# First x rows as four loads, per-channel constants turned by PE, and products ahead of PE's first projection

## The reference, cut to what matters

```python
# x: [4, 512, 512], ctx: [4, 512, 256]; DI = 512 channels, DS = 16 states, DC = 4 taps
z   = layernorm(x)                                   # used as the gate, per row
xi  = einsum('ed,bld->bel', in_proj_w, ctx)          # in-projection
xc  = depthwise_conv(xi, conv_w, 4 taps)             # taps: conv_w [512, 4]
u   = silu(xc + conv_b[None, :, None])
xdbl = einsum('ke,bel->bkl', x_proj_w, u)            # rows: dt_lo 16, B 16, C 16
delta = softplus(einsum('er,brl->bel', dt_proj_w, dt_lo) + dt_proj_b)
A = -exp(A_log)
# for each step t: state = state * exp(delta_t * A) + delta_t * u_t * B_t;  y_t = sum_n state * C_t
y = (y + D * u) * silu(z)
x = x + swapaxes(y, 1, 2)
# then x + ffn(layernorm(x)), with weights rounded to -1, 0, 1 by their mean and rows rounded to 8 bits
```

## Time and profile before

| what | value |
|---|---|
| time, median of 3 runs (range) | 584.99 us (584.41 to 585.54) |
| the profiled execution's own time | 586.31 us |
| its span, first to last instruction | 584.4 us |
| mean granted TensorE clock | 0.991 |
| busy: PE, DVE, ACT, POOL | 541.3, 540.5, 512.1, 464.5 us |
| chain that ended last, by engine | DVE 28%, PE 26%, ACT 17%, POOL 12%, issue 11%, DMA 5% |
| DMA busy share in the first four of 40 slices (14.6 us each), in tenths | 9, 9, 9, 2 |
| packets under 512 bytes | 41136 of 62194 |

### The profile page before, as it was taken

One profiled execution on the slowest core, in us unless ns is written; L12 is line 12 of the kernel. 1 busy time (PEld: TensorE's weight loads), 2 busy tenths in 40 slices (PEclk: granted clock), 3 DMA queues, 4 the chain that ended last, 5 costly groups with the idle time before them and its releaser, 6 DMA issues.

```text
span 584.4 us, 10287 instructions
## 1 busy us (share of the span) xinstructions
PE 541.3 (93%) x3667; PEld 404.7 (69%) x3684; DVE 540.5 (92%) x820; ACT 512.1 (88%) x755; POOL 464.5 (79%) x184
## 2 busy tenths in 40 slices
PE   5898987999999999999999888998889999999996
PEld 2335476899998989989999888995334444444442
DVE  3999979999999999999999999997998999999873
ACT  1899999999999999989999799998967868778673
POOL 4888374999999899999999999994564765666662
PEclk9999999999999999999999899899999999999998
DMA  9992690221112741127331194234532533424321
GB/s 285 407 364 73 230 309 11 56 65 64 55 55 91 163 117 65 59 63 202 88 98 55 55 228 168 62 128 106 104 65 63 109 81 78 112 65 97 94 54 55
DMA packets 62194, 68.65 MB, mean 117 GB/s; under 512 B 41136, under 2 KB 41136, under 8 KB 59968
## 3 DMA queue, kind: packets, MB, share of 16 engines
q1 hardware_dynamic: 59776, 63.59, 36.3%
q0 software_dynamic: 2368, 4.40, 4.5%
HBM read 50.02 MB, written 8.52 MB: 100 GB/s over the span
## 4 chain that ended last, share of the span: by engine, by line
DVE 28%; PE 26%; ACT 17%; POOL 12%; issue 11%; DMA 5%; SPq 0%; DVEq 0%; POOLq 0%; ACTq 0%
POOL arena L470 11%; ACT arena L682 8%; PE ps L1221 8%; PE ps L1205 6%; ACT arena L607 5%; DVE arena L808 5%; PE ps L1208 4%; PE ps L1263 4%; PE ps L1256 3%; DVE arena L897 3%; DVE arena L985 3%; DMA arena<-arena 2%; DVE bst_x L840 2%; DVE am L954 1%; DMA arena<-x 1%
## 5 line engine op out<-in xcount | busy, mean ns | idle before, releaser
L470 POOL TENSOR_TENSOR arena<-arena 128x2048 f32<-128x2048 f32 x63 | 286.4, 4592 | 13.2 <-DVE arena L897 11.1
L897 DVE TENSOR_TENSOR_SCAN arena<-arena,ps 128x512 f32<-128x512 f32 x256 | 286.7, 1197 | 2.0 <-ACT arena L682 0.5
L682 ACT ACTIVATE arena<-arena,a_neg 128x512 f32<-128x512 f32 x256 | 165.5, 712 | 9.5 <-DVE arena L897 9.2
L1221 PE MATMUL ps<-ident,arena 128*128 128x128 f32 x1024 | 156.0, 276 | 6.7 <-POOL arena L470 3.4
L1221 PEld LDWEIGHTS ps<-ident,arena 128*128 128x128 f32 x1024 | 121.2, 142 | 10.7 <-POOL arena L470 6.2
L504 POOL TENSOR_TENSOR arena<-arena 128x1024 f32<-128x1024 f32 x30 | 71.1, 2371 | 57.2 <-DVE arena L985 57.2
L1256 PE MATMUL ps<-arena 128*128 128x512 bf16 x504 | 112.9, 379 | 2.1 <-DVE arena L985 1.1
L1205 PE MATMUL ps<-arena 128*128 128x128 f32 x768 | 102.3, 276 | 3.4 <-ACT arena L607 2.1
L1208 PE MATMUL ps<-ident,arena 128*128 128x128 f32 x640 | 97.8, 277 | 5.2 <-DVE arena L897 2.9
L607 ACT ACTIVATE arena<-arena,bT 128x512 f32<-128x512 f32 x160 | 102.0, 711 | 0.0
L1205 PEld LDWEIGHTS ps<-arena 128*128 128x128 f32 x768 | 93.3, 192 | 5.2 <-ACT arena L607 2.3
(11 more groups left out here) (121 smaller groups left out, 578.1 us busy)
## 6 DMA issues: line engine op xcount, KB each, us to landing
arena<-w_all SPq DMA_DIRECT2D x16, 1024.0 KB, 9.2
arena<-c_rows SPq DMA_DIRECT2D x64, 256.0 KB, 3.2
arena<-x SPq DMA_DIRECT2D x4, 1024.0 KB, 15.8
w_ternary<-arena SPq DMA_DIRECT2D x8, 512.0 KB, 4.2
arena<-w_ternary SPq DMA_DIRECT2D x8, 512.0 KB, 5.0
arena<-x POOLq DMA_DIRECT2D x4, 1024.0 KB, 10.0
out<-arena SPq DMA_DIRECT2D x16, 256.0 KB, 2.0
arena<-ctx_t SPq DMA_DIRECT2D x4, 512.0 KB, 13.7
```

Of the source, the lines that this page charges most:

```text
L470: nc.gpsimd.tensor_tensor(hs[:, k % RING, :, :], hs[:, k % RING, :, :], c_bc[:, s:s + 1, :].to_broadcast([P, KE, L]), ALU.mult).then_inc(S ...
L682: nc.scalar.activation(dA[:, s, i, :], delta_u[:, b, 0, i, :], ACT.Exp, scale=a_neg[:, i, n:n + 1]).then_inc(S["dA_ready"], 1)
L897: nc.vector.tensor_tensor_scan(out=hs[:, k % RING, i, :], data0=dA[:, k % 2, i, :], data1=ps[:, 4 + i, :], initial=0.0, op0=ALU.mult, op1= ...
L1221: last = mm(ps[:, c, i * P:(i + 1) * P], hs[:, k % RING, i, c * P:(c + 1) * P], ident[:], start=(n == 0 and i == 0), stop=(n == DS - 1), i ...
```

## The change

Five things are changed, all of them in the head.

1. SP no longer loads `cw` and `cb`, and loads x for b = 0 as four transfers of 256 KB, one for each block of 128 rows, each with a semaphore (`x0_loaded`). `x_stats(0)` waits for them one by one.
2. ACT issues three loads at its start: taps, bias and D, laid out as rows (4 partitions with 512, 128 and 128 contiguous values, 12 rows in all). PE turns them with six transposes behind `conv(0, 0)` into PSUM bank 7, and DVE copies them from there into one tile, `chan`, behind `x_stats(0)`. ACT's `last_tap`, DVE's `conv` and POOL's `skip` read `chan`. ACT's first `last_tap` therefore waits for DVE's copy.
3. PE does `keep_warm(9)` ahead of `conv(0, 0)`. It waits only for `dve_consts`, and DVE writes `ones` and `magic` first now.
4. POOL's loads come later: `xp_t` as one transfer with 192 bytes in a piece, then `dt_t` and `dt_b`, all behind `x_power(0)`; `a_log` behind `x_power(2)`. `d_skip` is no longer loaded by POOL. Two copies on POOL behind `x_norm(0)` put `xp_t` where `project` reads it.
5. Waits for `proj_ready`, `proj_loaded` and `a_loaded` stand where their readers are.

```diff
-            load(cw[:], conv_w.rearrange("(k p) n -> p k n", p=P), "conv_loaded")
-            with nc.allow_non_contiguous_dma("one column for each channel"):
-                load(cb[:], conv_b.rearrange("(k p) -> p k", p=P), "conv_loaded")
-            load_x(0)
+            for k in range(KE):
+                sp.dma_start(x_all[:, k, :], x_v[:, 0, k, :]).then_inc(x0_loaded[k], 16)
...
-            xp_v = xp_t.rearrange("(k p) n -> p k n", p=P)
-            pool.wait_ge(S["started"], 2)
-            load(xp_s[:, :, 0:DR], xp_v[:, :, 0:DR], "proj_loaded")
-            load(xp_s[:, :, B_AT:XD], xp_v[:, :, DR:DR + 2 * DS], "proj_loaded")
...
-            load(a_neg[:], a_log.rearrange("(k p) n -> p k n", p=P), "consts_loaded")
-            with nc.allow_non_contiguous_dma("one column for each channel"):
-                load(dsk[:], d_skip.rearrange("(k p) -> p k", p=P), "consts_loaded")
...
             x_power(0)
+            load(xp_raw, xp_t.rearrange("(k p) n -> p k n", p=P), "xp_loaded")
+            pool.wait_ge(S["started"], 2)
+            for j in range(2):
+                at = j * XD
+                load(dt_s[at:at + DR, j, :], dt_t, "proj_loaded")
+                load(dt_s[at + DR:at + DR + 1, j, :], dt_b.rearrange("(a n) -> a n", a=1), "proj_loaded")
             x_norm(0)
+            pool.wait_ge(S["xp_loaded"], 16)
+            nc.gpsimd.tensor_copy(xp_s[:, :, 0:DR], xp_raw[:, :, 0:DR]).then_inc(S["proj_ready"], 1)
+            nc.gpsimd.tensor_copy(xp_s[:, :, B_AT:XD], xp_raw[:, :, DR:]).then_inc(S["proj_ready"], 1)
             x_power(1)
             x_norm(1)
             x_power(2)
+            load(a_neg[:], a_log.rearrange("(k p) n -> p k n", p=P), "a_loaded")
...
-            act.wait_ge(S["conv_loaded"], 16 * 2)
...
+            for at, src in ((0, conv_w.rearrange("(k p) n -> k (p n)", p=P)),
+                            (TAPS * P, conv_b.rearrange("(k p) -> k p", p=P)),
+                            ((TAPS + 1) * P, d_skip.rearrange("(k p) -> k p", p=P))):
+                act.dma_start(chan_rows[:, at:at + src.shape[1]], src).then_inc(S["chan_loaded"], 16)
             act.preload_act_table_set("silu_and_others")
+            act.wait_ge(S["chan_ready"], 1)
             last_tap(0, 0)
...
+            step(nc.vector.memset(ones[:], 1.0))
+            nc.vector.memset(magic[:], MAGIC).then_inc(S["dve_consts"], 1)
             nc.vector.memset(xp_s, 0.0).then_inc(S["started"], 1)
             nc.vector.memset(dt_s, 0.0).then_inc(S["started"], 1)
...
             x_stats(0)
+            dve.wait_ge(S["chan_psum"], 1)
+            nc.vector.tensor_copy(chan[:], ps[:, 7, 0:(TAPS + 2) * KE]).then_inc(S["chan_ready"], 1)
+            dve.wait_ge(S["chan_ready"], 1)
             conv(0, 0)
...
+            pe.wait_ge(S["dve_consts"], 1)
+            keep_warm(9)
             pe.wait_ge(S["in_loaded"], 16)
             conv(0, 0)
+            pe.wait_ge(S["consts_set"], 1)
+            pe.wait_ge(S["chan_loaded"], 16 * 3)
+            for i in range(TAPS + 2):
+                rows = chan_rows[:, i:TAPS * P:TAPS] if i < TAPS else chan_rows[:, i * P:(i + 1) * P]
+                last = nc.tensor.transpose(ps[:, 7, i * KE:(i + 1) * KE], rows, ident[0:KE, 0:KE])
+            last.then_inc(S["chan_psum"], 1)
             conv(0, 1)
```

43 lines of the change are left out of this document (22 added, 21 removed).

## The result

The changed kernel takes 588.71 us (median of 17 runs, 586.57 to 592.23), the kernel before in the same comparison 585.51 us (17 runs, 584.41 to 588.15). The ratio is 1.0057, 95% interval [1.0038, 1.0075]: 3.2 us slower, where 2.0 us faster was forecast. The runs of the changed kernel also lie further apart, 5.7 us instead of 3.7.

What follows compares the result with a forecast made beforehand. The head was taken as fixed DVE work starting when x lands, with landings second. DVE's conv 2.0 us sooner, passed to the scan, gave 584.3 from the profiled 586.31, or 583.0 us against the median 584.99; range 582.2 to 584.9.

Steps and rivals of the forecast that it cites:

- The landing of x, the projection, the transposes: Head: DVE's first statistics near 7.5 us, first projection 3.70 us, six transposes 0.9 us, DVE's conv at 11.9 to 12.0.
- The rule against the quarters: Head, loads of x: taken one after the other, four quarters need 2.6 us each, the last near 12.2, no gain.
- The clock comes late: Rival, chance 0.20: PE's level rises only during or after its first projection in the head; 584.4 us between its cases.
- Does it get through?: Head up to the scan: landings of x (2.2 us for b = 2) and ACT (2.5 us) let the whole 2.0 us through.
- the sum: Main case, chance 0.62: 2.0 us gained at DVE's first conv reaches the scan; 583.0 us, own range 582.3 to 583.6.
- They end by 5.8 and cost nothing: Start of PE: the nine unread products finish before ctx_t lands at 6.25 us, so their cost is zero.
- POOL's late loads: POOL between x_power(0) and x_norm(0): about 3 us of loads, hidden since PE reads the normed x after 70 us.
- the case of late constants: Rival, chance 0.05: the rows of taps, bias and D land at 12.3 to 13.8 us in the head; 585.4 to 586.9.
- F: Follow-up theory, no chance given: added PE instructions move 16 KB program fetches into DMA transposes, lengthening POOL's feed-forward products (weighs).

Runs made afterwards that it cites:

- the version with the old position: Changed kernel with POOL's loads early, fewer later unread products and four idle instructions, PE's program where it stood before: 584.99 us against 584.99, ratio 1.0002.
- the three pairs: POOL's loads late against early: kernel before 586.34 against 585.09 us, changed kernel 588.71 against 586.53, changed without nine unread products 586.43 against 585.78.
- position 49: Kernels whose edit adds 49 instructions to PE's program ahead of the last part (0: none), such as the changed one, 588.71 us, and 49 idle instructions, 588.09.
- -12: Three later unread products (12 instructions) taken from the kernel before, 586.42 us, ratio 1.0015, and from the version with the old position, 586.22 us, ratio 1.0025.

## Why the prediction was wrong

**The landing of x, the projection, the transposes: right.** The first quarter of x was there at 7.45, PE was at its higher level (3.67 us), the transposes took 0.76 us, all within 0.5 us of the forecast. The conv started at 12.22 instead of the 11.9 to 12.0: `ctx_t` let PE begin at 6.70 rather than 6.25, and the copy waited 0.33 us for PE. The rule against the quarters did not hold: they landed at 7.43, 8.12, 8.77 and 9.44 us, some 0.67 apart, and not 2.6. The Trainium skill gives its fixed 2.0 us (DMA: Bandwidth & Descriptors, Anatomy of one DMA) for DMAs that GpSimd issues, and these are SP's.

**"The clock comes late": a true rival, not the cause.** Three of ten profiles had it, against the 0.20 that I gave; these are ten kernels with one profile each. The Trainium skill's rule that the moment of the transition differs from run to run (TensorE: Matmul & The Clock Gate, What's actually happening) agrees with them, but can't be told from a difference between the kernels. It costs the lead, and by the forecast's own sum can hardly make a kernel slower than before.

**"Does it get through?": here it failed, twice.** Up to the scan the sum had 2.0 us and measured 1.0. The lead began at 1.69, and x for b = 2 allowed 1.42, where I had given it 2.2. The landings lead by 2.0 us up to the second weight piece (15.78 against 17.81), but by 1.2 for x of b = 1 and 0.8 for x of b = 2 (31.21 against 31.98), and between them POOL's loads come in, issued from 12.20 on and landed by 21.46; the sum had 0.4 us for these. With POOL's loads early x of b = 2 lands at 30.9 to 31.2 as well: pieces that were only moved gain it nothing. Then came 0.3 us where POOL's `skip` and DVE's rounding overlap, a term that the sum didn't have, and 0.1 in the store. ACT, to which I had given 2.5 us, was in nobody's way, though its weight piece came 0.97 us sooner and not the 1.6. From the scan on, the sum had no term at all. I had read the chain from its start up to 93 us and took the rest as fixed, and the rest was 491 us long. A lead of 1.0 us was worth nothing at its end, in the profile of after (-0.1 at the fourth batch), and it does not show in the version with the old position (same time as before with a scan 1.1 us sooner, where the interval leaves at most 0.6 us of gain). What takes it back between the scan and the weighs is not shown.

**The unread products and the moved loads were costed at nothing: this made it slower.** "They end by 5.8 and cost nothing" is the step that failed, though the place that hides them was right: PE had nothing to do there. The cost lies elsewhere, in the length of PE's program. 49 idle instructions alone give 2.8 of the 3.2 us; one alone gives 1.6. POOL's late loads, which the prediction called hidden, are worth 0.2 to 1.8 us by the three pairs. With a lead that is worth nothing the two make 3.0 to 4.6 us against 3.2 measured. They are not independent, since 1.2 of the 1.8 are weighs as well.

**Slips in the working.** PE's four times eight records were taken at 3.6 us where their row has 3.70, the end of `x_stats(0)` at 14.01 where the conv begins at 13.91, and the case of late constants reaches 586.9 in one place and 586.5 in the next. None of them bears on the result.

**What F explains, and what it doesn't.** Shown: fetches that meet transposes go with weighs that are 0.9 to 1.7 us longer than before. Not shown is where the rest of the 2.8 us of 49 idle instructions goes. In the profile of that kernel a part of it is a drop of PE's granted clock to 0.50 (1.2 GHz) at 80.5 us. Busy time of each engine at 80 to 95 us, then PE's granted clock, DMA share and GB/s, before and with 49 idle instructions:

```profile
80.00:95.00 15.00, 13.00 (x113) 12.12 (x112) 12.47 (x13) 14.04 (x23) 9.07 (x2) 1.00 0.44 147
```

```profile
80.00:95.00 15.00, 14.40 (x112) 13.65 (x109) 11.02 (x12) 12.14 (x18) 9.08 (x2) 0.89 0.44 143
```

PE turns z and du there at half speed, it is waited for, and the scan starts at 94.87 instead of 93.32. Four of twenty profiles have such a drop at 79 to 81 us (two of them at position 49, one at 0, one at -12), and three of these four start the scan at 94.9 to 95.3.

Are such drops more frequent in the changed kernel? The mean granted clock of every run is on record and says no: it averages 0.994 over the changed kernel's 17 runs and 0.994 over the 132 of the kernel before in the five later comparisons. In runs with 0.996 or more the medians are 586.84 (6 runs) and 585.14 (53), 1.7 us apart, as much as the weighs. In runs below that they are 589.80 (11) and 585.30 (79), 4.5 us apart. So what the weighs don't explain stands in the runs that spend more time at the lower clock, and a drop seems to cost the changed kernel more than the kernel before. The groups were made after the fact and come from several chips, so this is a lead and not a proof. The kernel with 49 idle instructions has 0.992 on average and no run at 0.996, so a part of its 2.8 us may be more drops.

The rest stays open: what a drop costs at which place, what POOL's late loads cost behind the head, and what the fetches do to the scan. From first scan to first weigh the profiles at the old position have 313.7 to 315.4 us, those at 49 have 314.8 to 315.5, too close to tell.

## What to carry to other kernels

A lead at the start is a gain only if the chain is followed to its end: look for the engine that sets the long middle part, and for what there is not tied to the lead. Instructions in idle time are not free in a long program: they move every later fetch of the engine's program, and in this kernel idle instructions alone were worth 1.6 us (one) and 2.8 us (49), as much as the edit under test. To measure an edit, hold the length of the program (add or remove idle instructions that cost nothing in their place), or measure several lengths. A tuned kernel may stand at a lucky position: none of the 15 kernels at other positions was faster than this one, though the four others at its position weren't either. When an edit shifts two engines against each other, look at what they now do at the same time: here DVE and POOL both slowed down where they met.

## What was not expected of the hardware

- One instruction of 0.11 us in PE's idle time moved a fetch of 16 KB by 2.7 us (491.1 to 488.4), made a DMA transpose land in 6.1 instead of 4.4 us, and went with a kernel 1.6 us slower (ratio 1.0024 [1.0011, 1.0037]), of which 1.0 us is in the weighs.
- During a fetch that meets the end of a transpose, packets of 4 bytes took 1.4 us.
- A look at a semaphore that was long set costs PE 0.11 us per instruction of two looks.
- Where POOL's 128x128 TENSOR_SCALAR instructions overlap DVE's 128x2048 rounding, four of them take 3.76 to 4.76 us instead of 2.35, and the rounding 1.47 to 1.62 instead of 1.21 (six profiles against fourteen).
- Eighteen unread records over 3.7 to 4.2 us, 0.8 to 1.7 us ahead of the first projection, had PE at its higher level in that projection in seven profiles of ten.
